# Parts of queries and keys kept in DRAM in the order of the partitions that read them

## What is computed

```python
# layer 0 (A): Q = x, K = V = ctx_1024
q = (Q @ Wq + bq).reshape(b, s, H, DH).transpose(0, 2, 1, 3)
...
out = ctx @ Wo + bo + Q          # then a layer norm with gamma, beta
# layer 1: tgt = layer 0's result, memory = ctx_1024
q, k, v = _linear(tgt, q_w, q_b), _linear(tgt, k_w, k_b), _linear(tgt, v_w, v_b)
tgt2 = _linear(_attention(q, k, v, tgt_mask), o_w, o_b)          # B
x = _layernorm(tgt + tgt2, ln1_g, ln1_b)
q, k, v = _linear(x, cq_w, cq_b), _linear(memory, ck_w, ck_b), _linear(memory, cv_w, cv_b)
tgt2 = _linear(_attention(q, k, v, None), co_w, co_b)            # C
x = _layernorm(x + tgt2, ln2_g, ln2_b)
tgt2 = _linear(relu(_linear(x, lin1_w, lin1_b)), lin2_w, lin2_b)
x = _layernorm(x + tgt2, ln3_g, ln3_b)
```

## Time and profile before

| | us |
|---|---|
| median of 3 runs | 1944.6 (1944.24 to 1947.28) |
| the profiled execution, whole | 1945.19 |
| its span, first to last instruction | 1943.4 |
| TensorE busy in the span | 1853.8 |

### The profile page before, as it was taken

How to read it: one execution, slowest core, us unless ns; L and a number is a source line. 1 busy time by engine, 2 the same in 40 slices (tenths; PEclk the granted TensorE clock), 3 DMA queues, 4 the chain that set the end, 5 groups by cost and what they waited for, 6 DMA issues and landing times. The chain is left out here.

```text
span 1943.4 us, 39350 instructions
## 1 busy us (share of the span) xinstructions
PE 1853.8 (95%) x12608; PEld 1434.5 (74%) x12608; DVE 1326.3 (68%) x5194; ACT 1192.7 (61%) x3985; POOL 987.8 (51%) x1014
## 2 busy tenths in 40 slices
PE   8999999999999999999999999999999999998887
PEld 6677677777777777777777777777777777776565
DVE  3565776766768677676766768677676766757863
ACT  3374766656566666666656566666666656566852
POOL 2252645546465454645546465454645546455742
PEclk9999999999999999999999999999999999999989
DMA  8244343261622618143261622618143271625420
GB/s 209 78 75 69 71 71 56 51 109 35 102 35 64 86 35 125 35 71 56 52 109 35 99 38 66 85 35 126 35 71 56 52 109 35 103 34 87 72 44 12
DMA packets 147528, 135.49 MB, mean 70 GB/s; under 512 B 23424, under 2 KB 142976, under 8 KB 147328
## 3 DMA queue, kind: packets, MB, share of 16 engines
q1 hardware_dynamic: 144208, 132.97, 38.7%
q10 hardware_dynamic: 3120, 0.01, 0.1%
HBM read 90.99 MB, written 41.94 MB: 68 GB/s over the span
## 5 line engine op out<-in xcount | busy, mean ns | idle before, releaser
L1063 POOL TENSOR_TENSOR prob<-prob,recip 128x512 f32<-128x512 f32 x768 | 793.0, 1054 | 818.2 <-DVE recip L983 817.5
L800 ACT ACTIVATE prob<-prob,ext 128x256 f32<-128x256 f32 x1536 | 758.5, 502 | 16.1 <-DVE ext L972 16.1
L807 ACT ACTIVATE prob_t<-ps_t 128x512 f32<-128x512 f32 x384 | 228.9, 596 | 445.6 <-PE ps_t L710 445.4
L710 PE MATMUL ps_t<-ident,prob 128*128 128x128 f32 x3072 | 408.1, 275 | 16.8 <-DVE prob_t L988 15.9
L710 PEld LDWEIGHTS ps_t<-ident,prob 128*128 128x128 f32 x3072 | 355.8, 141 | 62.7 <-issue 20.9
L988 DVE COPY prob_t<-ps_t 128x512 f32<-128x512 f32 x384 | 262.2, 683 | 170.8 <-PE ps_t L710 170.0
L800 ACT ACTIVATION_READ_ACCUMULATOR prob<-prob,ext 128x1 f32 x1536 | 298.9, 195 | 0.0
L972 DVE CUSTOM_DVE_ANT_0 prob<-ps_s,mask_a 128x256 f32<-128x256 f32 x512 | 187.0, 421 | 110.9 <-PE ps_s L693 110.8
L972 DVE CUSTOM_DVE_ANT_0 prob<-ps_s,mask_b 128x256 f32<-128x256 f32 x512 | 186.1, 419 | 56.3 <-PE ps_s L693 55.7
L972 DVE CUSTOM_DVE_ANT_0 prob<-ps_s,zero 128x256 f32<-128x256 f32 x512 | 185.9, 418 | 38.9 <-PE ps_s L693 37.9
L693 PE MATMUL ps_s<-k_ctx,q 64*128 64x256 f32 x1024 | 146.1, 404 | 8.6 <-DVE ext L972 2.9
(11 more groups left out here) (87 smaller groups left out, 2521.3 us busy)
## 6 DMA issues: line engine op xcount, KB each, us to landing
k_B<-k_parts_B SPq DMA_DIRECT2D x128, 128.0 KB, 5.1
q_B<-q_parts_B SPq DMA_DIRECT2D x128, 128.0 KB, 9.4
k_C<-k_parts_C SPq DMA_DIRECT2D x120, 128.0 KB, 4.8
q_C<-q_parts_C SPq DMA_DIRECT2D x120, 128.0 KB, 4.8
k_parts_C<-k_hl SPq DMA_DIRECT2D x16, 512.0 KB, 2.9
k_parts_B<-k_hl SPq DMA_DIRECT2D x16, 512.0 KB, 2.9
q_parts_B<-q_hl SPq DMA_DIRECT2D x32, 256.0 KB, 2.4
q_parts_C<-q_hl SPq DMA_DIRECT2D x32, 256.0 KB, 9.5
```

The costliest lines, as they stand in the source:

```text
L710: last = nc.tensor.transpose(two(ps_t[e])[:, kt, qt * P:(qt + 1) * P], src[:, e, qt, kt * P:(kt + 1) * P], ident[:, :])
L800: last = nc.scalar.activation(tile, tile, ACT.Exp, bias=ext[:, slot, e, t:t + 1], scale=-1.0, accum_out=sums[:, slot, e, t:t + 1])
L807: nc.scalar.activation(prob_t[:, body.slot(step, PT_RING), 0], two(ps_t[0]), ACT.Copy).then_inc(pt_act[s], 1)
L1063: nc.gpsimd.tensor_tensor(rows, rows, recip[:, slot, e].unsqueeze(2) .to_broadcast([P, TT, TOK]), ALU.mult).then_inc(normed[s], 1)
```

## The change

- In DRAM, `k_parts` and `q_parts` get the shape (half, part, row, pair, token), the order of the partitions of `k4` and `q4`. All four parts are stored, so high and low are written twice each. A save is four DMAs of 256 KB, a read one DMA of 1 MB: 128 partitions, 8 KB in a row each.
- So that a save can keep its partitions in order, the columns of four weights of layer 1 (`q`, `k`, `cq`, `ck`) are sorted at the start. They are loaded into tiles that are still free, and GpSimd copies them in 16 copies (`sort_weights`) in round 1, between two of its multiplies. The four biases are sorted by eight DMAs from DRAM to DRAM with 4 bytes a piece, then loaded.
- `qc` is split into `k_hl`, so the order of users of that tile is `ks`, `qc`, `kc`.
- Saves and reads are steps of their own in the list: the read of queries comes one place after their save, the read of B's keys one place after their save. Loading, storing, saving cross keys and reading cross values move one or two places later.

TensorE's and ScalarE's lists are the same, and VectorE's differ only in the tile of `qc`.

```diff
-        ("A", 1): [job("qs"), dma("q", "B"), job("q", 1)],
...
+        ("A", 1): [dma("k", "B"), job("qs"), dma("save q", "B"), job("q", 1)],
+        ("A", 2): [dma("q", "B"), job("x2T"), job("v", 0)],
...
+        unsorted = {"q": v1["B"], "k": v1["C"], "cq": ctx1["B"], "ck": ctx1["C"]}
...
-        k_parts = {"B": nc.dram_tensor("k_parts_B", (1, 2, D, TOK), F32),
-                   "C": nc.dram_tensor("k_parts_C", (BATCH, 2, D, TOK), F32)}
-        q_parts = {s: nc.dram_tensor("q_parts_" + s, (2, D, TOK), F32) for s in "BC"}
+
+        k_parts = {"B": nc.dram_tensor("k_parts_B", (1, 2, PARTS, DH1, PAIRS, TOK), F32),
+                   "C": nc.dram_tensor("k_parts_C", (BATCH, 2, PARTS, DH1, PAIRS, TOK), F32)}
+        q_parts = {s: nc.dram_tensor("q_parts_" + s, (2, PARTS, DH1, PAIRS, TOK), F32) for s in "BC"}
...
-                sp.dma_start(k_parts["C"][bass.ds(b, 1)].rearrange("b a (d p) t -> p b (a d) t", p=P),
-                             k_hl[:, :, :, :].rearrange("p a d t -> p (a d) t").unsqueeze(1)
-                             ).then_inc(k_saved["C"], 16)
+                for part in range(PARTS):
+                    sp.dma_start(k_parts["C"][bass.ds(b, 1), :, part].rearrange("b e r c t -> (r c) b e t"),
+                                 k_hl[:, part % 2].unsqueeze(1)).then_inc(k_saved["C"], 16)
...
-                sp.wait_ge(k_saved[s], count(b, 16, 16))
+                sp.wait_ge(k_saved[s], count(b, 16 * SAVES, 16 * SAVES))
                 if s != home:
                     sp.wait_ge(scored["B"], count(b, HEADS, HEADS))
                 elif s == "C" and not (isinstance(b, int) and b == 0):
                     sp.wait_ge(scored["C"], count(b - 1, HEADS, HEADS))
-                kept = k_parts[s][:, :] if s == "B" else k_parts[s][bass.ds(b, 1)]
-                by_pair = kept.rearrange("b a (e c r) t -> e a r (b c) t", e=2, r=DH1)
-                for part in range(4):
-                    for e in range(2):
-                        sp.dma_start(k4[home][rows_of(e, part), :, :].bitcast(F32), by_pair[e, part % 2]
-                                     ).then_inc(spread_k[s], 16)
+                kept = k_parts[s][0] if s == "B" else k_parts[s][bass.ds(b, 1)]
+                rows = "e a r c t -> (e a r) c t" if s == "B" else "b e a r c t -> (b e a r) c t"
+                sp.dma_start(k4[home][:, :, :].bitcast(F32), kept.rearrange(rows)).then_inc(spread_k[s], 16)
+
+            def save_queries(s, b):
+                parts = q_hl if s == "B" else k_hl
+                for part in range(PARTS):
+                    if part % 2 == 0:
+                        sp.wait_ge((q_high[s], taken["qs" if s == "B" else "qc"])[part // 2], count(b, 1, 1))
+                    sp.dma_start(q_parts[s][:, part].rearrange("e r c t -> (r c) e t"), parts[:, part // 2]
+                                 ).then_inc(q_saved[s], 16)
 
             def spread_queries(s, b, home):
-                for a, split in enumerate((q_high[s], taken["qs" if s == "B" else "qc"])):
-                    sp.wait_ge(split, count(b, 1, 1))
-                    sp.dma_start(q_parts[s][a].rearrange("(d p) t -> p d t", p=P), q_hl[:, a, :, :]
-                                 ).then_inc(q_saved[s][a], 16)
-                if s == "B":
-                    spread_keys(s, b, home)
-                for part in range(4):
-                    if part % 2 == 0:
-                        sp.wait_ge(q_saved[s][part // 2], count(b, 16, 16))
-                    for e in range(2):
-                        src = q_parts[s][part // 2].rearrange("(e c r) t -> e r c t", e=2, r=DH1)
-                        sp.dma_start(q4[home][rows_of(e, part), :, :].bitcast(F32), src[e]
-                                     ).then_inc(spread_q[s], 16)
+                sp.wait_ge(q_saved[s], count(b, 16 * SAVES, 16 * SAVES))
+                sp.dma_start(q4[home][:, :, :].bitcast(F32), q_parts[s].rearrange("e a r c t -> (e a r) c t")
+                             ).then_inc(spread_q[s], 16)
...
+            for n in sorted_bias:
+                for k in range(DT):
+                    sp.dma_start(sorted_bias[n][k].rearrange("(r c) -> r c", c=PAIRS),
+                                 io[f"{L1}{n}_b"].rearrange("(k c r) -> k r c", c=PAIRS, r=DH1)[k],
+                                 allow_slow_non_contiguous=True).then_inc(bias_sorted, 16)
...
+                    sp.dma_start(unsorted.get(n, w1[n])[:, :, :], wide(f"{L1}{n}_w")).then_inc(w_in["attn1"], 16)
...
+            for n in sorted_bias:
+                sp.wait_ge(bias_sorted, 16 * DT * len(sorted_bias))
+                sp.dma_start(col[n][:, :], sorted_bias[n].rearrange("k p -> p k"), allow_slow_non_contiguous=True
...
-                        pe.wait_ge(w_in["attn1"], 16 * (len(w1) + 2))
+                        pe.wait_ge(w_sorted, len(unsorted))
...
-                parts, high = (q_hl, q_high[s]) if name[0] == "q" else (k_hl, k_high[s])
+                parts = q_hl if name == "qs" else k_hl
+                high = (q_high if name[0] == "q" else k_high)[s]
                 if isinstance(b, int) and b == 0:
                     dve.wait_ge(w_in["small"], 16 * small)
 
                 past = body.earlier(step, 1, lambda x: x[0] == "J" and x[1] in
-                                    (("qs", "qc") if name[0] == "q" else ("ks", "kc")))
+                                    (("qs",) if name == "qs" else ("ks", "qc", "kc")))
                 if past:
                     (_, other, _, _), b0 = past
-                    s0 = "B" if other[1] == "s" else "C"
-                    for saved in q_saved[s0] if name[0] == "q" else [k_saved[s0]]:
-                        dve.wait_ge(saved, count(b0, 16, 16))
+                    saved = {"qs": q_saved["B"], "qc": q_saved["C"], "ks": k_saved["B"], "kc": k_saved["C"]}[other]
+                    dve.wait_ge(saved, count(b0, 16 * SAVES, 16 * SAVES))
...
+            def sort_weights():
+
+                pool.wait_ge(w_in["attn1"], 16 * (len(w1) + 2))
+                for n, w in unsorted.items():
+                    for d in range(DT):
+                        for m in range(2):
+                            last = nc.gpsimd.tensor_copy(
+                                w1[n][:, d, m * P:(m + 1) * P].rearrange("p (r c) -> p r c", r=DH1),
+                                w[:, d, m * P:(m + 1) * P].rearrange("p (c r) -> p r c", r=DH1))
+                    last.then_inc(w_sorted, 1)
+
             def job(body, step):
-                _, name, _, _ = step
+                _, name, i, _ = step
+                if body.present == {"x", "a"} and (name, i) == ("k", 3):
+                    sort_weights()
```

More of the change, by code:

```diff
@@ L214, in last_schedule @@
             [],
-            [ln("m2", "ln3"), io("m2", "store")],
-            [],
+            [ln("m2", "ln3")],
+            [io("m2", "store")],
             [job("m3", "oc")],
@@ L373, in program @@
         k_high = {s: sem("k_high_" + s) for s in "BC"}
-        q_saved = {s: [sem(f"q_saved_{part}_{s}") for part in ("high", "low")] for s in "BC"}
+        q_saved = {s: sem("q_saved_" + s) for s in "BC"}
         k_saved = {s: sem("k_saved_" + s) for s in "BC"}
@@ L391, in program @@
         column = lambda n: io[n].rearrange("(k p) -> p k", p=P)
+        sorted_bias = {n: nc.dram_tensor("bias_" + n, (DT, P), F32) for n in ("q", "k", "cq", "ck")}
         L0, L1 = "L0_xattn_", "L1_xattn_"
@@ L553, in _ @@
                         {"load": load, "store": store, "save_c": save_cross, "value_c": load_values}[step[1]](body, step)
-                    elif step[0] == "DMA" and step[1] == "save":
-                        save_keys(body, step)
-                    elif step[0] == "DMA" and step[1] == "k":
-                        spread_keys("C", body.batch(step), HOME.get(step[3], "C"))
                     elif step[0] == "DMA":
-                        spread_queries(step[2], body.batch(step), HOME.get(step[3], step[2]))
+                        what, s, b = step[1], step[2], body.batch(step)
+                        if what == "save k":
+                            save_keys(body, step)
+                        elif what == "save q":
+                            save_queries(s, b)
+                        else:
+                            (spread_keys if what == "k" else spread_queries)(s, b, HOME.get(step[3], s))
             sp.wait_ge(out_done, 16 * BATCH + 16)
```

71 lines of the change are left out of this document (34 added, 37 removed).

## The result

| | median, us | runs | lowest to highest |
|---|---|---|---|
| before | 1944.52 | 12 | 1940.32 to 1947.28 |
| after | 1949.81 | 12 | 1947.08 to 1952.42 |

The changed kernel takes 1.003 times the time of the one before, 95% interval 1.0023 to 1.0038: it is slower by 4.5 to 7.4 us. The forecast was 1942.0 with a range up to 1948.5; the result lies outside, on the other side. The profiled execution of after took 1949.13 us (span 1947.3), against 1945.19 (1943.4) before: 3.9 us more. Two executions of the experiments took far longer than the others of their kernel, 2223.39 us in e3 and 10390.69 us in e8; the ratios leave them out, the medians count them in. In what follows "late by" is the distance between the same instruction in the two traces.

A forecast was written before the change was run, and what follows sets the result against it. TensorE, busy 1853.8 of 1943.4 us, was taken as the bound. Profiled 1945.19 us less 1.01 (pause) less 1.55 (clock), start 0, gave 1942.6, so a median of 1942.0 us; range 1939.5 to 1948.5.

The forecast's parts named there:

- term (1) of the start: Eight bias-sorting DMAs ahead of the weights: later issues move by 3.8 to 8.6 us, 4 taken; cost nothing.
- Term (2): Start: big loads end near 56 us instead of 52.2; x_tok's transpose at 59.5 has 0.4 us of cover, so untouched.
- the GpSimd rival: Strided weight-sorting copies cost a whole multiply each, delaying x_tok: 1949.6 us; chance 0.09, shared with a slow start.
- One sign of the list: Expected in the profile after, at the start: x_tok's transpose at 59 to 60 us.
- Term (3): Start: GpSimd's 16 weight-sorting copies take 0.41 us each, 6.5 us, hidden in 10.12 us of idleness; cost nothing.
- The reads: Each 1 MB read of parts as one DMA over 128 partitions: some 5 us from issue to landed.
- The chain: Saves and reads in series, round at 174 us: q_C landed some 199 us, needed at 206.5, 7 us of cover.
- The 1.01 us and the clock: Before attention C's first scores, near 207 us: the 1.01 us pause goes; clock staying 1.00 afterwards gains 1.55 us.
- The shared tile: Cross queries' split into k_hl waits for the keys' saves, with 7.7 us of cover; cost nothing.
- the moved steps: Load, store and saving of cross keys and values move one or two places later in SyncE's list; cost nothing.
- the steady round: Middle of the kernel: a steady round stays at 116.6 us with the same pauses.
- the bytes: Bytes written to DRAM rise by 4 x 0.5 MB a batch, 33 MB.

The follow-up runs named there:

- e3: The kernel before with the eight sorting DMAs of biases added, their result unused: 1952.03 us, ratio 1.0049.
- e8: The changed kernel with the eight sorting DMAs issued by ScalarE, on its queue, behind its three bias loads: 1952.44 us, ratio 1.0051.
- e4: The kernel before with eight DRAM to DRAM DMAs added, each copying its 512 B in the order they lie, unsorted: 1943.14 us, ratio 1.0005.
- e9: The changed kernel with biases read from the input in sorted order straight into SBUF columns, without the eight DRAM to DRAM DMAs: 1941.67 us, ratio 0.9997.
- e11: The kernel before with eight stores of 128 x 4 B from SBUF to DRAM added at the place of the sorting DMAs: 1950.14 us, ratio 1.0035.
- e6: The changed kernel, all sorting kept, with the two 1 MB MLP weight loads issued behind the first batch's saves: 1943.62 us, ratio 1.0005.
- e2: The changed kernel without GpSimd's 16 copies, four weights left in the old column order: 1950.34 us, ratio 1.0041.
- e1: The changed kernel without the eight sorting DMAs, the four biases loaded unsorted: 1941.16 us, ratio 0.9994.
- e5: The changed kernel with four sorting DMAs instead of eight, the cross biases loaded unsorted: 1942.19 us, ratio 0.9996.
- e7: The changed kernel with the eight sorting DMAs issued by GpSimd at its start, on its own queue: 1958.91 us, ratio 1.0085.

## Why the prediction was wrong

**The step that failed is the cost of the eight sorting DMAs, term (1) of the start.** It counted SyncE's time to issue them, from plain issues and column loads, with 3.8 and 8.6 us as its ends and 4 as its value. The list was late by 13.8 us. The counted part was about right: in e4, with the same issue times, the first column load is issued at 25.03, 4.5 us late, and nothing is lost. What wasn't counted, and so stood at nothing, is the time for which the pieces hold up the transfers behind them: at the first column load after is at 34.34, 9.3 us behind e4, and at the MLP weights at 51.9 against 39.8, 12.0 us or 1.5 for each DMA of 512 B. The nearest row that was used, a column load of 4-byte pieces, goes the other way, into SBUF, and e9 shows that this direction is cheap. The bound therefore wasn't one: the trace of before has no write of small pieces to DRAM at all, and the step took the price of a read for it.

What in the path is held isn't shown. It isn't the engines' time on the pieces themselves, which the trace has at 9 ns each.

The Trainium skill, "DMA: Bandwidth & Descriptors", section Specifications, says that below 512 B the DMA engine reads, modifies and writes. The runs agree in part: 4-byte pieces into DRAM (e3, e11) are slow, but 4-byte pieces into SBUF (e9) aren't, nor are pieces of 32 B into DRAM (e4), which are also below 512 B. No run here shows the reading and modifying itself.

**Term (2) had the right mechanism and the wrong input.** The big loads did end late and x_tok did stand behind them, with the 0.4 us of cover that was named; "at 8.6 it waits 2 us" was the right kind of sentence. With 13.8 us in it, the same sum gives 52.2 + 13.8 = 66.0 for the last load; 65.6 was measured, and x_tok behind it at 66.2. Then came what the step left out: the clock, at half in and behind the wait, for another 1.6 us. In the chances the start only shared the 0.09 of the GpSimd rival; though it held the largest unknown, it had no rival with a price of its own. The constants came later than the far end too, at 59.1 us against 55.4; e6 shows that this cost nothing that can be measured. One sign of the list was the right one: x_tok's transposes at 59 to 60 us, which came at 66.4.

**Term (3), GpSimd's copies:** 0.41 us each forecast, 0.34 to 0.35 measured, 5.5 us for 16, done 3.1 us ahead of the next multiply. Right, and e2 confirms it, though they began at 42.45 instead of 40.1, behind the late load of w_co.

**The reads:** 5 us from issue to landed forecast, 4.7 to 6.2 measured. **The chain:** q_C landed some 7 us ahead of its use by the forecast; in after it is issued at 205.2, lands at 210.1 and is used at 214.98, 4.9 us ahead. **The 1.01 us and the clock** behind them went as forecast: 1.01 + 1.55 = 2.56, against the 2.6 us that the traces show between 89 and 218 us. For the clock that is luck, as the next paragraph shows. **The shared tile, the moved steps, the steady round, the bytes** (written to DRAM 75.5 MB against 41.9): as forecast.

**What stays open.** That gain of 2.6 us is seen in the pair of traces, but the medians don't carry it. The four kernels that have the wide reads and no loss at the start (e1, e5, e9 and e6) stand at 0.9994, 0.9996, 0.9997 and 1.0005, from 1.2 us below before to 1.0 above, each interval with 1 in it; 2.6 us would be 0.9987. e4, which has the pause of 0.96 us at the same place, shows granted clock 1.00 behind it, and so makes up 1.6 us on the trace of before without the change. So the low clock there isn't in every execution, and the 1.55 us was a term that counts only for some. That leaves the pause of 1.01 us, 0.9995, which these intervals neither show nor exclude. How often the low clock occurs wasn't measured. Neither is any version here shown to be faster than the kernel before: e9 is the better form of this change, and equals it.

## What to carry to other kernels

A DMA has two prices here, the issue on its queue and the time for which its pieces hold up the transfers behind them, on other queues too; the second has no row until something like it has run, so a kind of transfer that the trace lacks (here small pieces written to DRAM) deserves a rival of its own, however few its bytes. Sort small tables on the way into SBUF, where 4-byte pieces were cheap, and never through DRAM. For a reordered layout, ask which part of it earns the gain: here it was the one DMA over 128 partitions, not the longer run by itself (one DMA of that kind in 1 KB pieces was not tried).

## What the runs showed of the hardware that was not expected

- Eight DMAs that write 128 x 4 B each to DRAM delay the first column load behind them by 13.8 us (after), 14.8 (e3) and 12.9 (e11, from SBUF), their issue included; as 16 pieces of 32 B each they delay it by 4.5 and land 0.2 us apart (e4). From GpSimd's queue they delay SyncE's as well: 6.13 us for one issue, while the eight land 2.9 us apart (e7).
- The pieces of 4 bytes take 9 ns each in the trace; it is packets of 1 KB behind them that take up to 2.5 us (after).
- 1024 pieces of 4 bytes read from DRAM into SBUF: eight landings some 0.65 us apart, SyncE's pace of issuing (e9).
- 1 MB over 16 partitions at a time: 0.93 us for 128 KB in 1 KB pieces, 1.0 us in 8 KB runs. In one DMA over 128 partitions: 4.8 us from issue to landed for the whole.
- TensorE's clock fell to 1.2 GHz within the 5.98 us wait and stayed there for 6.8 us. Behind a pause of about 1 us it fell in the trace of before and not in that of e4.
